# Fused LSTM, attention, GRU and mixture of experts on one core: the LSTM's products move ahead, and vector work, routing and some expert products change places

## The reference

```
y  = x  + attention(lstm(x,  h0=cond))        # causal, 16 heads of 64, latent width 32
out = y + moe(gru(y, h0=cond))                # 8 experts, 128 -> 512 -> 128, top 2 of softmax
lstm step:  a = x_t Wx + h Wh + b;  c = f*c + i*g;  h = o*tanh(c)
gru step:   z, r = sigmoid([x_t, h] W + b);  cand = tanh([x_t, r*h] Wh + bh)
            h_new = (1-z) h + z cand;  after every 4th step h = tanh(h_new Wp + bp)
```

## Time and profile before

| | |
|---|---|
| time, median of 3 runs | 589.99 us (588.25 to 590.3) |
| the profiled execution's own time | 591.56 us |
| its span, first to last instruction | 589.7 us |
| PE busy | 525.5 us (89%) |
| DVE busy | 424.1 us (72%) |
| ACT busy | 352.9 us (60%) |
| mean granted clock of PE | 0.93 |

### The profile page before, as it was taken

One profiled execution on the slowest core, in us unless ns is written; L12 is line 12 of the kernel. 1 busy time (PEld: TensorE's weight loads), 2 busy tenths in 40 slices (PEclk: granted clock), 3 DMA queues, 4 the chain that ended last, 5 costly groups with the idle time before them and its releaser, 6 DMA issues.

```text
span 589.7 us, 20148 instructions
## 1 busy us (share of the span) xinstructions
PE 525.5 (89%) x7315; PEld 483.4 (82%) x7356; DVE 424.1 (72%) x2402; ACT 352.9 (60%) x1297; POOL 33.6 (6%) x85
## 2 busy tenths in 40 slices
PE   7967887889789898989999989898999998889998
PEld 3736675888679898989888989898989988879998
DVE  4447678767776887878787878787879788664432
ACT  2235345775256676757676767676676767565562
POOL 6000000000000000000000000000000000000000
PEclk9679659699759999999999999999999999999999
DMA  8810101010100101010101010101101010100000
GB/s 204 327 15 6 20 1 20 3 13 10 16 11 6 16 5 17 12 20 3 19 12 17 7 15 16 12 10 12 16 14 13 4 17 13 18 1 3 11 7 10
DMA packets 75118, 14.32 MB, mean 24 GB/s; under 512 B 71411, under 2 KB 74111, under 8 KB 74638
## 3 DMA queue, kind: packets, MB, share of 16 engines
q1 hardware_dynamic: 74566, 11.96, 11.2%
q10 hardware_dynamic: 456, 1.08, 0.6%
HBM read 7.78 MB, written 1.05 MB: 15 GB/s over the span
## 4 chain that ended last, share of the span: by engine, by line
PE 68%; DVE 17%; issue 6%; ACT 6%; DMA 1%; SPq 1%; POOL 0%; DVEq 0%; ACTq 0%; POOLq 0%
PE pH L488 16%; PE pG L488 12%; PE pV L488 12%; PE pY L488 9%; PE pL L488 8%; PE pC L578 5%; PE pS L488 5%; ACT hid L864 2%; PE pC L488 2%; DVE latNlo L976 2%; DVE acc L1073 1%; DVE gB L1137 1%; DVE ghi L1140 1%; DVE glo L1143 1%; ACT gC L879 1%
## 5 line engine op out<-in xcount | busy, mean ns | idle before, releaser
L864 ACT ACTIVATE hid<-pH,b 128x256 f32<-128x256 f32 (+1 forms) x320 | 116.3, 433 | 3.9 <-PE pH L488 3.9
L488 PE MATMUL pY<-w,hid 128*128 128x128 f32 x608 | 85.1, 284 | 0.0
L488 PE MATMUL pH<-ghi,w1hi 128*128 128x256 f16 (+1 forms) x320 | 76.7, 254 | 9.1 <-ACT hid L864 7.3
L488 PE MATMUL pH<-ghi,w1lo 128*128 128x256 f16 (+1 forms) x320 | 77.0, 255 | 0.0
L488 PE MATMUL pH<-glo,w1hi 128*128 128x256 f16 (+1 forms) x320 | 76.9, 255 | 0.0
L488 PEld LDWEIGHTS pY<-w,hid 128*128 128x128 f32 x608 | 74.6, 193 | 0.2
L871 ACT ACTIVATE gT<-pG 128x32 f32<-128x32 f32 x128 | 24.7, 193 | 70.5 <-PE pG L488 70.3
L488 PE MATMUL pV<-w,hid 128*128 128x128 f32 x416 | 58.2, 283 | 0.0
L1124 DVE SCALAR_TENSOR_TENSOR gRZ<-gT,g 128x32 f32<-128x32 f32 x128 | 24.5, 191 | 46.6 <-ACT gT L871 46.0
L1137 DVE TENSOR_TENSOR gB<-gRZ,gC 128x16 f32<-128x16 f32 x128 | 22.5, 175 | 46.9 <-ACT gC L879 44.5
L879 ACT ACTIVATE gC<-pG 128x16 f32<-128x16 f32 x128 | 23.5, 183 | 52.9 <-PE pG L488 52.8
(11 more groups left out here) (177 smaller groups left out, 1569.6 us busy)
## 6 DMA issues: line engine op xcount, KB each, us to landing
w<-in_w SPq DMA_DIRECT2D x2, 2048.0 KB, 13.1
qbd<-qh SPq DMA_DIRECT2D x256, 16.0 KB, 1.9
out<-acc SPq DMA_DIRECT2D x16, 64.0 KB, 1.5
xT<-in_xT ACTq DMA_DIRECT2D x1, 960.0 KB, 8.2
hid<-in_WqT SPq DMA_DIRECT2D x1, 512.0 KB, 5.6
hid<-in_Wout SPq DMA_DIRECT2D x1, 512.0 KB, 10.3
lWh<-in_lWh SPq DMA_DIRECT2D x1, 256.0 KB, 2.8
lWx<-in_lWx SPq DMA_DIRECT2D x1, 256.0 KB, 3.1
```

Source lines behind the costliest of these rows:

```text
L488: return nc.tensor.matmul(o, lhsT=lhsT, rhs=rhs, start=start, stop=stop, skip_group_check=True)
L864: A(hid[:, e % NHID, c, 0:W], pH[half][:, W * at:W * (at + 1)], ACT.Gelu, bias=b1[:, e, c:c + 1], scale=1.0 / SP).then_inc(gelu, 1)
```

## The change

- PE: `l_step` stands right behind `g_step` in all steps, ahead of the candidate.
- ACT: lT comes right behind gT, then `setup` and the EXP table (now in phase 3), the GELUs of half 0, `pt_copy`, lC, and only then gC. `route_copy` moves from DVE to ACT. `low` is dropped: the routing's tanh takes the maximum as its bias.
- DVE: `cell` (lP, oK, lT) directly follows gRZ and gA. Then `maximum`, `combine` B, `add_x`, `pt_rest` (before gB now), `route_pick`, gB to glo, `hidden` (hhi, hfull, hlo), `invert`, and `between`, into which `lat_copy` and `q_rest` (one operation in place of four) move, behind `turn_values` and `combine` A. `turn_latents` comes one phase later.
- Routing begins in phase 1 in place of 2, and `route_first` in phase 2.
- Slot A's products of phases 2 and 3 go to pC, the bank of the transposes, in place of pV.
- One slot-B product of each visit moves from phase 6 to phase 0 (steps 38, 46 and so on to 40, 48 and so on).

```diff
-             (37, "B", 3, 0), (38, "B", 3, 1), (42, "A", 4, 0), (42, "B", 4, 1), (43, "A", 5, 0), (43, "B", 5, 1),
-             (44, "A", 6, 0), (44, "B", 6, 1), (45, "B", 7, 0), (46, "B", 7, 1))
+             (37, "B", 3, 0), (40, "B", 3, 1), (42, "A", 4, 0), (42, "B", 4, 1), (43, "A", 5, 0), (43, "B", 5, 1),
+             (44, "A", 6, 0), (44, "B", 6, 1), (45, "B", 7, 0), (48, "B", 7, 1))
...
 def route_stages(i):
-    at = GS * i + (26 if i < NG - 1 else 25)
-    if i > 12:
-        return at, at + 1, at + 2, at + 3, at + 3
-    return at, at + 1, at + 2, at + 6, at + 8
+    at = GS * i + 25
+    return (at, at + 1, at + 2, at + 3, at + 3) if i > 12 else (at, at + 1, at + 3, at + 7, at + 9)
+
+def down_bank(k, slot):
+    return "Y" if slot == "B" else "C" if k % TB in (2, 3) and k < LAST else "V"
...
-TO_EXP = [TB + O_S] + [k + 1 for k, half in UPS if half == 0 and (k + 1, 0) not in UPS and k < T]
+TO_EXP = [TB + O_S] + [k + 2 for k, half in UPS if half == 0 and (k + 1, 0) not in UPS and k < T]
...
-            def turn_probs(n):
+            def turn_probs(n, k):
                 pe.wait_ge(exp_done, 4 * (n + 1))
-                pe.wait_ge(q_lo, HG * (n // NU + 1))
+                pe.wait_ge(q_lo, n // NU + 1)
                 if n:
                     pe.wait_ge(pt_split, n)
+                if downs_before(k, "C"):
+                    pe.wait_ge(acc_done, downs_before(k, "C"))
...
                     if at == 0:
+                        bank = down_bank(k, slot)
+                        if downs_before(k, bank):
+                            pe.wait_ge(acc_done, downs_before(k, bank))
+                        if bank == "V":
                             pe.wait_ge(on_done, count(lambda j: unit_at(j, O_V), k))
                             copied(k)
+                        elif bank == "C":
+                            pe.wait_ge(q_lo, count(latents_at, k))
                         else:
                             pe.wait_ge(lat_done, count(latents_at, k + 1))
...
                 if 0 <= g < T:
                     g_step(g)
-                if t < LAG:
+                if t < T:
                     l_step(t)
...
                     g_candidate(g)
-                if LAG <= t < T:
-                    l_step(t)
...
+            def route_copy(n):
+                m, tg = visit_of(n)
+                act.wait_ge(r_mm, n + 1)
+                if n >= 2:
+                    act.wait_ge(r_ranked, n - 1)
+                A(lg[:, n % 2, :], pV[:, 256:256 + E], ACT.Copy, scale=0.5).then_inc(r_copy, 1)
+                if slots_used(m, tg):
+                    act.wait_ge(stored[2 * (m % 3) + tg], 16 * slots_used(m, tg))
+                A(acc[:, m % 3, tg, :], pV[:, 384:512], ACT.Copy).then_inc(r_copy, 1)
...
                 if k in FIRST:
                     n = FIRST[k]
-                    act.wait_ge(r_low, n + 1)
-                    A(th[:, n % 2, :], low[:, n % 2, :], ACT.Tanh, scale=0.5).then_inc(r_th, 1)
+                    act.wait_ge(route[n % 2], 10 * (n // 2) + 1)
+                    A(th[:, n % 2, :], lg[:, n % 2, :], ACT.Tanh, bias=lmax[:, n % 2, 0:1]).then_inc(r_th, 1)
+                if k in ROUTES:
+                    route_copy(ROUTES[k])
...
             def between(k):
-                if unit_at(k, O_T) is not None:
+                if unit_at(k, O_T) is not None and k < LAG:
                     pt_rest(unit_at(k, O_T))
                 if unit_at(k, O_V) is not None:
                     normalise(unit_at(k, O_V))
...
                 if (k, "A") in DOWN_AT:
                     combine(k, "A")
+                if latents_at(k) is not None:
+                    lat_copy(latents_at(k))
+                if latents_at(k - 1) is not None:
+                    q_rest(latents_at(k - 1))
...
+                if t < T and k >= LAG:
+                    cell(t)
+                if unit_at(k - 1, O_S) is not None:
+                    maximum(unit_at(k - 1, O_S))
+                if t < T and k < LAG:
+                    cell(t)
                 if (k - 1, "B") in DOWN_AT:
                     combine(k - 1, "B")
+                if period_at(k) is not None:
+                    add_x(period_at(k))
                 if k >= LAG:
-                    after_latents(k)
-                if unit_at(k - 1, O_S) is not None:
-                    maximum(unit_at(k - 1, O_S))
+                    setup_late(k)
+                if unit_at(k, O_T) is not None and k >= LAG:
+                    pt_rest(unit_at(k, O_T))
```

More of the change, by code:

```diff
@@ L117, in gelus_of, with downs_before @@
     return max(n for (vm, ve, h), n in GELUS.items() if (vm, ve) == (m, e))
-def downs_before(k, slot):
-    return max([ORDER[d] + 1 for (at, sl), ds in DOWN_AT.items() if sl == slot and at < k for d in ds], default=0)
+def downs_before(k, bank):
+    return max([ORDER[d] + 1 for (at, slot), ds in DOWN_AT.items() if down_bank(at, slot) == bank and at < k for d in ds], default=0)
 def count(at, upto):
@@ L245, in build @@
         lmax = sb("lmax", [128, 2, 1])
-        low = sb("low", [128, 2, E])
         th = sb("th", [128, 2, E])
@@ L871, in _ @@
                     A(gT[:, :, :], pG[:, 0:2, g % GS, :], ACT.Tanh, scale=1.0 / SP).then_inc(g_tanh, 1)
+                if t < T:
+                    act.wait_ge(l_gates, t + 1)
+                    A(lT[:, 0:4, :], pL[:, :, t % GS, :], ACT.Tanh, scale=1.0 / SP).then_inc(l_tanh, 1)
+                if k >= LAG:
+                    setup(k)
+                if k in TO_EXP:
+                    A(spare[:, 1:2], still[:, 0:1], ACT.Exp)
                 for m, e, chunks in UPS.get((k - 1, 0), []):
@@ L876, in _ @@
                     pt_copy(unit_at(k, O_T))
+                if t < T:
+                    act.wait_ge(l_c, t + 1)
+                    A(lC[:, :], lT[:, 4, :], ACT.Tanh, scale=0.5).then_inc(l_tc, 1)
                 if 0 <= g < T:
@@ L879, in _ @@
                     A(gC[:, :], pG[:, 2, g % GS, :], ACT.Tanh, scale=1.0 / SP).then_inc(g_c, 1)
[L880 to L883, removed]
+                if unit_at(k, O_T) is not None and not early:
                     pt_copy(unit_at(k, O_T))
-                if unit_at(k - 1, O_S) is not None and k >= LAG:
+                if unit_at(k - 1, O_S) is not None:
                     exps(unit_at(k - 1, O_S))
@@ L891, in _ @@
                     A(gp, pG[:, 3, (g + 1) % GS, :], ACT.Tanh, scale=1.0 / SP).then_inc(g_p, 1)
[L892 to L899, removed]
+                if k < LAG:
+                    setup(k)
                 if k in TO_GELU:
                     A(spare[:, 0:1], still[:, 0:1], ACT.Gelu)
-                if k in TO_EXP:
-                    A(spare[:, 1:2], still[:, 0:1], ACT.Exp)
                 if latents_at(k) is not None:
@@ L964, in q_rest @@
                 dve.wait_ge(q_hi, p + 1)
[L965 to L968, removed]
+                V.scalar_tensor_tensor(qh[:, p % 2, :, 1, :, :],
+                                       pC[:, :].rearrange("p (g s b) -> p b g s", g=HG, b=B), 1.0 / SP,
+                                       qh[:, p % 2, :, 0, :, :], ALU.mult, ALU.subtract).then_inc(q_lo, 1)
             def turn_latents(p, whole_t, turned):
@@ L1013, in add_x @@
                                 ALU.add).then_inc(x1_done, 1)
[L1015 to L1019, removed]
-                if slots_used(m, tg):
-                    dve.wait_ge(stored[2 * (m % 3) + tg], 16 * slots_used(m, tg))
-                V.tensor_copy(acc[:, m % 3, tg, :], pV[:, 384:512]).then_inc(r_copy, 1)
             def route_first(n):
@@ L1107, in setup_late, with cell, hidden @@
                     V.scalar_tensor_tensor(w1lo[:, e, :], w1[:, e, :], SW, w1hi[:, e, :], ALU.mult, ALU.subtract).then_inc(set_w1, 1)
-            def after_latents(k):
-                setup_late(k)
-                if latents_at(k) is not None:
-                    lat_copy(latents_at(k))
-                if latents_at(k - 1) is not None:
-                    q_rest(latents_at(k - 1))
-                if period_at(k) is not None:
-                    add_x(period_at(k))
+            def cell(t):
+                dve.wait_ge(l_tanh, t + 1)
+                V.scalar_tensor_tensor(lP[:, :, :], lT[:, 0:2, :], 1.0, lT[:, 3:5, :], ALU.add, ALU.mult).then_inc(l_mul, 1)
+                V.tensor_scalar(oK[:, :], lT[:, 2, :], SH / 2, SH / 2, ALU.mult, ALU.add)
+                dve.wait_ge(l_mul, t + 1)
+                V.scalar_tensor_tensor(lT[:, 4, :], lP[:, 1, :], 0.5, lP[:, 0, :], ALU.mult, ALU.add).then_inc(l_c, 1)
+            def hidden(t):
+                dve.wait_ge(l_tc, t + 1)
+                V.tensor_tensor(hhi[:, t + 1, :], oK[:, :], lC[:, :], ALU.mult).then_inc(l_hi, 1)
+                V.tensor_tensor(hfull[:, :], oK[:, :], lC[:, :], ALU.mult).then_inc(l_h, 1)
+                dve.wait_ge(l_h, t + 1)
+                V.tensor_tensor(hlo[:, t + 1, :], hfull[:, :], hhi[:, t + 1, :], ALU.subtract).then_inc(l_lo, 1)
             for k in range(STEPS):
```

(2 more changed lines are left out.)

58 lines of the change are left out of this document (17 added, 41 removed).

## The result

The changed kernel takes 622.38 us (median of 4 runs, 621.07 to 625.29) against 590.0 us before: a ratio of 1.0562, with a 95% interval of 1.0519 to 1.0606. It is slower, and the forecast was 615 in a range of 594 to 642. The profiled execution took 621.07 us, its span is 619.3.

The account below looks back on a forecast made before the run. PE was taken as the bound (29.26 of 31.27 us a repetition), DVE not far behind. 24 us for latT waits, 6 for other phases, -3 light steps, -2 tail: +25 on 591.56, 616.6, so 615 as median; range 594 to 642.

Parts of the forecast that it names:

- Phase 0: The moved slot-B product waits for late latT (+3.9 us): PE idle 1.8, step 2.2 us longer, 11 steps, 24 us.
- Phase 6 gives nothing back: Without the 1.0 us product phase 6 stays near 3.97 us, since ACT's table load ends it; bounds 0 to 1.0.
- Phases 1 and 2: 1.19 us of routing waits won, but gain eaten by late tanh, gRZ and queries: 8.63 to 8.7 us.
- Phases 3 to 5: Slot B waits for the later `combine`, 0.9, 0.1 and 0.6 us: 11.19 to 11.5 us, 0.3 more.
- my rival of the full queue: DVE operations with new neighbours lose 0.08 us each: 2.4 us a repetition, 25 us in all, 640; chance 0.17.
- Phases 6 and 7: Expert halves wait for GELUs 0.2 to 0.3 us later, since lT stands ahead: 7.73 to 7.95 us, 0.2 more.
- The sum of a repetition: Eight steps, phases 0 to 7: 5.9 + 8.7 + 11.5 + 7.95 = 34.05 us against 31.27.
- Outside the repetitions: Light steps 18 to 29, without experts: -3 us, bounds -8 and +2; tail: -2 us as routing waits go.
- The clock fell: Rival: phases 0 and 1 at half clock in ten repetitions, 16 us more, 631; chance 0.13.
- My own sign of being wrong: Listed under wrong: a granted clock under 1.00 after slice 13, beside early latT, phase 6 at 3, repetitions at 30 us.
- The row's price for the table load: Load at the start of phase 3 takes 1.28 + 0.2 us; only 0.5 shows ahead of gB, step's end unmoved.
- the change does what it says: Rival: phase 0 costs nothing, routing waits bring 10.6 + 5.0 us, light steps 3: 571 us; chance 0.12.

Follow-up runs that it names:

- run 2: Changed kernel with `lat_copy` early, right behind the cell in phase 0, nothing else moved: 598.0 us, ratio 1.012.
- run 1: Changed kernel with the slot-B product back in phase 6, all else as changed: 596.74 us, ratio 1.0094.
- run 4: Kernel before with only the slot-B product moved from phase 6 to phase 0, `lat_copy` staying early: 600.12 us, ratio 1.0144.
- run 12: Changed kernel with `q_rest` early, right behind the cell in phase 1, nothing else moved: 622.55 us, ratio 1.056.
- run 7: Changed kernel with `route_first` and the routing's tanh in phase 3 instead of phase 2: 623.72 us, ratio 1.0557.
- run 5: Kernel before with routing from phase 1, slot A of phases 2 and 3 in pC, `route_first` in phase 3, queues otherwise unreordered: 578.44 us, ratio 0.9785.
- run 6: Changed kernel with `combine` of slot B ahead of the cell, nothing else moved: 625.13 us, ratio 1.0584.
- run 8: Changed kernel with the product back in phase 6, `lat_copy` and `q_rest` early, `combine` B ahead of the cell, `route_first` in phase 3: 590.71 us, ratio 0.9992.
- run 9: The kernel of run 8 with PTlo (`pt_rest`) back behind `hidden`, as before: 584.4 us, ratio 0.9879.
- run 10: The kernel of run 9 with the EXP table loaded at the end of phase 2 again: 583.67 us, ratio 0.9863.

## Why the prediction was right

- **Phase 0, right and the largest term.** Predicted: latT at +3.9, PE idle for 1.8 us, the step 5.9 us, in 11 steps, 24 us. Measured: +3.88, 1.74 us in the view, 6.02 us, 11 waits (nine of 1.7 us, one of 2.4 in step 40, one of 1.4 in step 128); taking latT early gave 24.4 us back (run 2), taking the product away 25.6 (run 1).
- **Phase 6 gives nothing back, right.** Runs 1 and 4 show it with the product and without: 3.90 against 3.91, 3.97 against 3.97 us.
- **Phases 1 and 2, right in size, half right in cause.** Predicted 8.7, measured 8.34 us. The routing's tanh on ACT did wait for the maximum (18.0 us in 15 waits), and PE paused ahead of the scores until the queries came (run 12 removes it); but neither is worth anything alone (runs 7 and 12), because the time came back in a neighbouring step. "The gain is eaten" holds for the changed order only: in the old order the same two waits bring 12 us if `route_first` stays in phase 3 (run 5).
- **Phases 3 to 5, mis-sized.** Predicted 11.5, measured 11.85 us. The term in the sum was the wait for `combine`, put at 0.9, 0.1 and 0.6. It was 0.77 in phase 3 and 0.52 in phase 5, and run 6 shows that taking it away frees next to nothing. PTlo ahead of gB I had taken at nothing (ghi later, hidden earlier by as much). Once the waits are mended it costs 0.56 us in these three phases (12.09 against 11.53, runs 8 and 9): DVE's queue holds g back. That is the mechanism of my rival of the full queue, at a quarter of its 2.4 us a repetition.
- **Phases 6 and 7, about right**: 7.95 against 7.79 us, 0.06 us more than before where I had 0.2.
- **The sum of a repetition** came out 0.05 us from the measured one (34.05 against 34.00), and this is in part luck: phases 1 and 2 missed by 0.36 us one way, phases 3 to 5 by 0.35 the other.
- **Outside the repetitions, mis-sized.** For steps 56 to 127 the sum was 9 x 2.8 = 25 us, and 25.9 were measured, of which 1.4 are the clock in step 88. All else, with the waits of steps 40 and 128 in it, was to come out at nothing: -3 for the light steps, -2 for the tail. Measured: 3.7 us. Steps 18 to 29 became 1.8 us longer where I had them shorter by 3 (their granted clock was 0.68 against 0.73 before, so what the new order does there is not separated from the clock), steps 30 to 55 grew by 3.8 and the tail by 2.1; against that, step 18 began 3.9 us earlier, which I had not foreseen. That is the 4.5 us between my 616.6 and the profiled 621.07.
- **The rivals.** The clock fell, but once and briefly: 3.41 us at half clock in step 88, 1.4 us in all, against the 16 us that I had put on ten repetitions. My own sign of being wrong, a granted clock under 1.00 after slice 13, did show, though the page's row of slices is too coarse to show it. The eight other steps of the nine with an idle stretch of 1.7 us kept 1.00; run 4, which has no such wait, had a fall of 3.4 us in step 59, and runs 7 and 12 had two each. So the length of the idle stretch alone does not decide, and what does is not shown. (The Trainium skill, "TensorE: Matmul & The Clock Gate", section "Why this matters for your kernels", warns of long idle gaps between bursts of matmuls; here the trace has a fall behind one of nine gaps of equal length.) The row's price for the table load held as a price: runs 9 and 10 differ by 0.7 us in all. That the step's end would not move did not: with the load in it phase 3 is 0.66 us longer and phase 2 0.65 shorter. (By the drain of the Trainium skill's "ScalarE: Activation LUTs", "What ACT_TABLE_LOAD costs", I had estimated 12 us in all. No such drain shows: in run 4 the load of 398.17 begins 0.02 us behind the activation ahead of it, and the next activation 0.01 behind the load.) That the change does what it says is true for one part alone, the routing.
- **What stays open.** Run 10 (new order, waits mended) is 0.46 us a repetition behind run 5 (old order). By the windows of the nine repetitions 0.21 of them is PE idle (1.48 against 1.27 us) and 0.25 PE busy. Step by step the new order loses 0.29 in phase 3 and 0.22 in phase 5, and wins 0.25 in phase 2; in its waits stand PE's transposes for `combine` of slot A in pC (4.7 us in 11 waits, 1.9 in 7 in run 5). Which edit of the order costs it was not tried. Nor was the start taken apart. gT of step 18 comes at 59.7 us in the changed kernel and at 63.0 in run 6, at 63.7 before and at 65.7 in run 4, so kernels whose first 18 steps are the same differ by 3.3 and 2.0 us, and of the 3.9 us an unknown part is one execution against another.

## What to carry to other kernels

When work is moved into a step, look up every semaphore that its bank or buffer waits for, and find the producer's place in its own queue: here a copy of 0.25 us, moved behind the rest of its step's vector work in the step that also got a product, cost 24 us. Work taken out of a step returns nothing if another engine's queue ends that step. And where the engines have little time free, do not judge a wait by its length in the view: three edits that each removed a visible wait gained nothing alone, and the same three, with `lat_copy` early, won 6 us together on the kernel of run 1 (run 8 against run 1). But split a bundle of edits to find the part that pays: the routing alone, in the old order, makes this kernel 2.15% faster (0.9785, interval 0.9744 to 0.9827).

## What the runs showed of the hardware

- A gap in the view understates what a wait costs PE: it counts from the end of the last product, which lies 0.16 us behind the point at which the next could have begun. Step 96 lost 1.91 us in run 2 where the wait it removed shows 1.74.
- PE's clock can fall from 2.4 to 1.2 GHz in the middle of busy steps: in step 88 it fell 0.21 us after PE had begun again behind an idle stretch of 1.74 us, and stayed there for 3.41 us, which made the step 1.4 us longer. In the eight other steps from 56 to 120 with an idle stretch of 1.7 us it stayed at 2.4 GHz.
- A table load takes 1.28 us and the next activation starts 0.01 to 0.02 us behind its end: GELU in run 4 (398.17 and 399.46), EXP in phase 3 of the changed kernel (399.63 and 400.93).
